# A four-part layer kernel on one core: the feed-forward part's layer norm begun inside the token mixing, its router by blocks, its chosen weights spread by a load

## The reference, cut to what matters

```python
x = x + _L0_attn_ref(_layernorm(x, axis=-1), ...)
x = x + _L0_ffn_ref(_layernorm(x, axis=-1), ...)
...
def _L0_ffn_ref(hidden_states, Wr, br, W1, b1, W2, b2, A1, B1, A2, B2):
    ...
    probs = jax.nn.softmax(x @ Wr + br, axis=-1)
    w, idx = jax.lax.top_k(probs, K)
    combine = jnp.einsum('tk,tke->te', w, jax.nn.one_hot(idx, E, dtype=x.dtype))
    base_h1 = x @ W1 + b1
    t1 = jnp.einsum('td,erd->ter', x, A1)
    l1 = jnp.einsum('ter,efr->tef', t1, B1) * SCALING
    a = gelu_new(base_h1[:, None, :] + l1)
    ca = a * combine[:, :, None]
```

## Time and profile before

| | us |
|---|---|
| median of three executions | 2739.33 |
| lowest, highest | 2738.68, 2741.82 |
| the profiled execution, its time | 2752.23 |
| the profiled execution, its span | 2750.2 |
| busy in the span: PE, DVE | 2630.2 (96%), 2046.9 (74%) |
| busy in the span: ACT, POOL | 1621.7 (59%), 2140.3 (78%) |
| mean granted PE clock | 0.978 of full |

### The profile page before, as it was taken

The page is one execution under the profiler, slowest core; times in us unless marked ns, Lnnn a source line. Parts: engine busy times, 40 slices in busy tenths (PEclk is TensorE's granted clock), DMA queues, the critical chain, the costliest instruction groups (busy, mean ns, idle before and its releaser), DMA issues. The chain is left out here.

```text
span 2750.2 us, 32506 instructions
## 1 busy us (share of the span) xinstructions
PE 2630.2 (96%) x11020; PEld 1874.6 (68%) x11021; DVE 2046.9 (74%) x2916; ACT 1621.7 (59%) x1891; POOL 2140.3 (78%) x1106
## 2 busy tenths in 40 slices
PE   7986999899999999999999999999999999997898
PEld 2333677667777777777777777777777777765665
DVE  6766556578888888888888888888888888886111
ACT  2223323367767776776777677767767767774122
POOL 2543588479988998998899899889989988997233
PEclk9997899999999999999999999999999999999999
DMA  2001456200000000000000000000000000005421
GB/s 68 0 0 53 108 169 167 72 12 5 9 4 20 8 5 16 5 8 5 20 8 5 16 4 9 5 16 8 8 16 4 9 4 9 1 20 142 169 61 46
DMA packets 76126, 90.52 MB, mean 33 GB/s; under 512 B 9310, under 2 KB 64865, under 8 KB 75970
## 3 DMA queue, kind: packets, MB, share of 16 engines
q1 hardware_dynamic: 72994, 81.30, 10.3%
q0 software_dynamic: 2976, 7.22, 0.8%
HBM read 62.39 MB, written 27.02 MB: 33 GB/s over the span
## 5 line engine op out<-in xcount | busy, mean ns | idle before, releaser
L1925 DVE TENSOR_TENSOR at_top<-at_psum_s,at_top 128x512 f32<-128x512 f32 x960 | 662.7, 690 | 215.5 <-ACT at_prob L1832 194.0
L1832 ACT ACTIVATE at_prob<-at_psum_s 128x1024 f32<-128x1024 f32 x512 | 521.4, 1018 | 452.2 <-PE at_psum_s L932 449.0
L2053 POOL TENSOR_TENSOR at_p_lo<-at_prob,at_p_hi 128x1024 fp32r<-128x1024 f32 x256 | 616.3, 2408 | 2.0 <-ACT at_p_hi L1846 2.0
L1914 DVE TENSOR_TENSOR at_prob<-at_prob,at_psum_m 128x1024 f32<-128x1024 f32 x512 | 603.5, 1210 | 0.0
L1838 ACT ACTIVATE at_prob<-at_prob 128x1024 f32<-128x1024 f32 x512 | 537.7, 1050 | 9.9 <-DVE at_prob L1914 6.7
L2082 POOL TENSOR_TENSOR at_acc<-at_acc,at_prob 128x1024 f32<-128x1024 f32 x189 | 453.1, 2397 | 82.8 <-ACT at_prob L1838 73.0
L1747 PE MATMUL at_psum_o<-at_prob,at_v 128*128 128x512 f32 x1024 | 483.4, 594 | 1.8 <-DVE at_oT_lo L1946 1.4
L2086 POOL TENSOR_TENSOR at_acc<-at_acc,at_prob 128x1024 f32<-128x1024 f32 x189 | 454.3, 2404 | 0.0
L930 PE MATMUL at_psum_s<-at_q_hi,sw_gate_up_hi 128*128 128x512 f32 x1024 | 403.4, 394 | 5.1 <-DVE sw_gate_up_lo L1906 5.1
L932 PE MATMUL at_psum_s<-at_q_hi,sw_gate_up_lo 128*128 128x512 f32 x1024 | 401.6, 392 | 0.0
L931 PE MATMUL at_psum_s<-at_q_lo,sw_gate_up_hi 128*128 128x512 f32 x1024 | 401.4, 392 | 0.0
(11 more groups left out here) (350 smaller groups left out, 4486.9 us busy)
## 6 DMA issues: line engine op xcount, KB each, us to landing
ef_gate_up<-in_ef_gate_up SPq DMA_DIRECT2D x8, 1024.0 KB
at_wq_split<-lf_pieces SPq DMA_DIRECT2D x8, 512.0 KB, 2.9
at_wk_split<-lf_pieces SPq DMA_DIRECT2D x8, 512.0 KB, 4.8
at_wv_split<-lf_pieces SPq DMA_DIRECT2D x8, 512.0 KB, 2.9
at_wo_split<-lf_pieces SPq DMA_DIRECT2D x8, 512.0 KB, 4.5
ef_down<-in_ef_down SPq DMA_DIRECT2D x8, 512.0 KB
ef_rows_in<-ef_zeros SPq DMA_DIRECT2D x23, 128.5 KB, 9.0
ef_rows<-ef_rows_in SPq DMA_DIRECT2D x23, 128.5 KB, 2.2
```

The lines of the kernel that those rows point to most:

```text
L1832: nc.scalar.activation(pair(u, c, half), psum_s[:, 2 * half:2 * half + 2, :], ACT.Copy).then_inc(kept, 1)
L1914: nc.vector.tensor_tensor(part, part, psum_m[:].unsqueeze(1).to_broadcast([P, 2, BT]), ALU.subtract).then_inc(shifted, 1)
L1925: nc.vector.tensor_tensor(top[:, u % 2, :], psum_s[:, t, :], top[:, u % 2, :], ALU.max).then_inc(maxed, 1)
L2053: nc.gpsimd.tensor_tensor(p_lo[:, at, :], part, p_hi[:, at, :].bitcast(F32), ALU.subtract).then_inc(p_lo_ready, 1)
```

## The change

The layer norm of blocks 0, 1 and 2 moves into the last three steps of the token mixing, as calls of `BlockNorm`. Statistics of block 0 come at the end of step 3; its deviation, inversion and (on ACT) normalised rows in step 4. The statistics of blocks 1 and 2 come in step 5 on DVE, their deviations on ACT after its loop, their inversions and normalised rows on DVE around the two last `add_out`. The normalised rows lie in the tile that later holds `weights`.

The Block of the layer norm is gone. The router's Block takes block 3's norm, the turns of all blocks, the splits into `x_hi` and `x_lo`, and the router's matmuls by blocks. Four small loads are issued first under a semaphore of their own and seven large ones behind them; POOL splits the router's weights after the small ones and `w1` and `b1t` after the large ones.

`chosen` holds only the one-hot rows. The two chosen weights of each token are turned by one transpose, copied to `weightT` (32 partitions, 128 columns), stored to DRAM by SP as `weight_rows`, and loaded back as two rows of 2048 numbers, each broadcast to 128 partitions. So PE has three spread matmuls per block, not five, and ACT two copies, not four. For blocks 2 and 3 POOL makes the two products with the first hits.

```diff
+    def normalise_on_vector(self, dve, b, rows):
+        nc, ln = self.nc, self.ln
+        dve.wait_ge(ln.rstd_ready, self.stds + b + 1)
+        for j in range(TPB):
+            i = b * TPB + j
+            nc.vector.tensor_scalar(rows[:, j, :], self.x_tok[:, i, :], self.mean_var[:, i, 0:1],
+                                    self.rstd[:, i:i + 1], ALU.subtract, ALU.mult).then_inc(ln.norm_ready, 1)
...
+        eps = next_norm.eps
...
+            next_norm.begin()
...
                         mixes, scans, norms = b < NB, 0 <= a < NB, 0 <= g < NB
+                        if s == NB:
+                            next_norm.deviation(act, 0)
                         for n in range(NM):
...
+                        if s == NB:
+                            next_norm.normalise(act, 0, next_rows(0))
+                    next_norm.deviation(act, 1)
+                    next_norm.deviation(act, 2)
...
                             whole(g)
+                        if s == NB + 1:
+                            next_norm.statistics(dve, 1)
...
                             if norms and n == 0:
                                 centre(g)
+                            if s == NB and n == 1:
+                                next_norm.invert(dve, 0)
+                            if s == NB + 1 and n == 0:
+                                dve.wait_ge(added, 2 * 3)
+                                next_norm.statistics(dve, 2)
...
                                 normalise(g)
                         if scans:
                             own_part(a)
+                        if s == NB - 1:
+                            dve.wait_ge(added, 2)
+                            next_norm.statistics(dve, 0)
+                        if s == NB + 1:
+                            next_norm.invert(dve, 1)
+                            next_norm.normalise_on_vector(dve, 1, next_rows(1))
                         if norms:
                             add_out(g, 0)
+                        if s == NB + 1:
+                            next_norm.invert(dve, 2)
+                            next_norm.normalise_on_vector(dve, 2, next_rows(2))
+                        if norms:
                             add_out(g, 1)
...
-    NQ = 4 * E
+    NQ = 2 * E
...
+                small = (
+                    (router_a1[:], w["lf_router_a1"].rearrange("(c p) n -> p c n", p=P)),
+                    (br[:], w["lf_br"][0, :].partition_broadcast(P)),
+                    (order[:], w["c_order"][0, :].partition_broadcast(P)),
+                    (choose[:], w["c_choose"]),
+                )
...
+                    (b2[:], w["lf_b2"][0, :].partition_broadcast(P)),
+                )
+                N_SMALL = 16 * len(small)
...
+                def turn_psum(b):
+                    return [banks[:, b % 2 * NC + c, :] for c in range(NC)]
+
+                def first_low(b):
+
+                    return "pool" if b >= 2 else "vector"
+
+                def low_done(b):
+                    return sum(2 if first_low(k) == "pool" else 4 for k in range(b + 1))
+
                 with nc.Block() as block:
+                    @block.sync
+                    def _(sp):
+                        for dst, src in small:
+                            sp.dma_start(dst, src).then_inc(small_moved, 16)
+                        for dst, src in loads:
+                            sp.dma_start(dst, src).then_inc(loaded, 16)
+                        sp.wait_ge(small_moved, N_SMALL)
+                        sp.wait_ge(chosen_copied, 1)
+                        sp.dma_start(weight_rows, weightT[:]).then_inc(small_moved, 16)
+                        sp.wait_ge(small_moved, N_SMALL + 16)
+                        flat = weight_rows.rearrange("(j i) p -> j (i p)", j=2)
+                        for j in range(2):
+                            sp.dma_start(weights[:, j, :], flat[j, :].partition_broadcast(P)).then_inc(small_moved, 16)
+                        sp.wait_ge(small_moved, N_SMALL + 48)
+                        sp.wait_ge(loaded, 16 * len(loads))
+
...
+                        pool.wait_ge(small_moved, N_SMALL)
...
+                        pool.wait_ge(loaded, 16 * len(loads))
...
+                        for b in range(NB):
+                            tok = bass.ts(b, BT)
+                            if first_low(b) == "pool":
+                                pool.wait_ge(spread_copied, 2 * b + 1)
+                                pool.wait_ge(t1_lo_ready, b + 1)
+                                nc.gpsimd.tensor_tensor(low_hi[:, 0, tok], t1_hi[:, tok].bitcast(F32), hits[:, 0, tok],
+                                                        ALU.mult).then_inc(split_steps, 1)
+                                nc.gpsimd.tensor_tensor(low_lo[:, 0, tok], t1_lo[:, tok].bitcast(F32), hits[:, 0, tok],
+                                                        ALU.mult).then_inc(split_steps, 1)
...
+                        def turn(b):
+                            if b >= 2:
+                                pe.wait_ge(ln.lo_copied, own_norm.copied + NC * (b - 1))
+                            own_norm.turn(pe, b, own_rows(b), turn_psum(b))
...
+                        def router(b):
+                            pe.wait_ge(ln.lo_copied, own_norm.copied + NC * (b + 1))
+                            if b == 0:
+                                pe.wait_ge(split_steps, 2)
...
+                        turn(0)
+                        turn(1)
+                        router(0)
+                        turn(2)
+                        router(1)
+                        turn(3)
+                        router(2)
+                        router(3)
+                        low_rank(0)
+                        pe.wait_ge(logitsT_copied, NB)
+                        for i in range(NT):
+                            last = nc.tensor.transpose(logits[:, i, :], logitsT[:, bass.ts(i, P)], ident[0:E, 0:E])
+                        last.then_inc(logits_ready, 1)
+                        for b in range(1, NB):
+                            low_rank(b)
                         pe.wait_ge(chosen_ready, 1)
+                        nc.tensor.transpose(banks[0:2 * NT, 0, 0:P], weight[:].rearrange("p j i -> p (j i)"),
+                                            ident[:]).then_inc(chosen_psum, 1)
...
+                            if Q_BANK(b) == 0:
+                                pe.wait_ge(chosen_copied, 1)
...
-                            pe.wait_ge(chosen_copied, 2 * b + 2)
-                            for k in range(5):
-                                n = 5 * b + k
...
+                                    ob, ok = divmod(n - 8, 3)
                                     if ok == 2:
-                                        pe.wait_ge(low_steps, 4 * ob + 4)
+                                        pe.wait_ge(low_steps, low_done(ob))
                                     else:
-                                        pe.wait_ge(spread_copied, 4 * ob + (ok + 1 if ok < 2 else ok))
-                                out = banks[:, (1 + n) % 8, :]
-                                if k < 3:
-                                    last = nc.tensor.matmul(out, choose_r[:, k, :], chosenT_r[:, tok], start=True, stop=True)
-                                else:
-                                    last = nc.tensor.matmul(out, weigh[:, k - 3, :], chosenT[:, tok], start=True, stop=True)
-                                last.then_inc(spread_psum, 1)
+                                        pe.wait_ge(spread_copied, 2 * ob + ok + 1)
+                                nc.tensor.matmul(banks[:, (1 + n) % 8, :], choose_r[:, k, :], chosenT[:, tok],
+                                                 start=True, stop=True).then_inc(spread_psum, 1)
...
+                        own_norm.deviation(act, 3)
+                        own_norm.take_hi(act, 0, turn_psum(0))
+                        own_norm.normalise(act, 3, own_rows(3))
+                        for b in range(1, NB):
+                            own_norm.take_hi(act, b, turn_psum(b))
...
+                        act.wait_ge(chosen_psum, 1)
+                        nc.scalar.activation(weightT[:], banks[0:2 * NT, 0, 0:P], ACT.Copy).then_inc(chosen_copied, 1)
                         for b in range(NB):
-                            tok = bass.ts(b, BT)
-                            act.wait_ge(chosen_psum, b + 1)
-                            for dst in (chosenT, chosenT_r):
-                                nc.scalar.activation(dst[:, tok], banks[0:NQ, Q_BANK(b), :],
-                                                     ACT.Copy).then_inc(chosen_copied, 1)
+                            act.wait_ge(chosen_psum, b + 2)
+                            nc.scalar.activation(chosenT[:, bass.ts(b, BT)], banks[0:NQ, Q_BANK(b), :],
+                                                 ACT.Copy).then_inc(chosen_copied, 1)
...
-                            for k in (0, 1, 3, 4):
-                                n = 5 * b + k
```

(41 more changed lines are left out.)

167 lines of the change are left out of this document (34 added, 133 removed).

## The result

The changed kernel takes 2722.26 us (median of 4 runs, 2721.14 to 2723.30), the kernel before on the same chip 2739.01 (4 runs, 2736.57 to 2741.82): ratio 0.9938, 95% interval 0.9922 to 0.9954. A later pair on another chip (e9) gives 2723.29 against 2738.40, ratio 0.9945 (0.9932 to 0.9958); one of e9's six executions, of 6808 us, is left out of that ratio. The profiled execution of the changed kernel took 2721.14 with a span of 2719.3.

What follows compares the result with a forecast made beforehand. Took a hand-over chain between token mixing and main loop, no engine full, as the bound: 1.8 us later, then 41.5 us where it was 58.0, 14.7 less, 2739.33 to 2724.6; range from 2718.5 to 2732.

Steps and rivals of the forecast that it cites:

- case A: Router chain: DVE waits for POOL's splits of w1 and b1t; 2724.6 us, own range 2722 to 2728, chance 0.58.
- the seam's gain: Third token-mixing step's first residual add to main loop's first matmul, 97.92 us before: claimed 14.7 us less.
- Step 1: Token mixing with the norm inside: ends 1.8 us later, from 0.4, 0.5 and 0.9.
- Step 2: From token mixing's end to the router's logits: logits at about 259.5, 8.1 us earlier than before.
- Step 3: Router chain meeting POOL's splits: two-input DVE instructions wait for whole POOL instructions; chosen_ready at 269.3, bounds 265.5 to 270.8.
- equal sharing: Router chain beside POOL, other reading: chain at most 1.3 us longer, total within 1.5 us of the free-running rival's.
- Step 4, compute: Router's end, turns, spreads and products on PE, ACT, DVE and POOL: from 269.3 to 281.5 to 282.3.
- Step 4, load: Router's end, weights stored and loaded back as two 1 MB broadcasts at 300 GB/s: landed at 281.5.
- C: Weight loads: broadcasts at half rate end last, landing at 288.7; total 2731.3 us, chance 0.12.
- D: Weight loads: landing after 296.7, slower than before; 2752.2 us at 60 GB/s, chance 0.03.
- A sign of being wrong: Main loop's first matmul to the span's end: forecast wrong if its 2453.2 us changed.

Runs made afterwards that it cites:

- e9: Changed kernel run again, unedited, on another chip: 2723.29 us, ratio 0.9945 to the kernel before.
- e1: Kernel before the change run again, unedited, for its profile: 2737.71 us (one run).
- e4: Changed kernel with the norm of blocks 0 to 2 moved out of token mixing to the router's Block: ratio 0.9952 to the kernel before.
- e7: Changed kernel with w1 and b1t loaded and split early, and the norm taken out of token mixing: ratio 0.9966 to the kernel before.
- e2: Changed kernel with w1 and b1t loaded first and split by POOL once those two landed: ratio 0.9922 to the kernel before.
- e3: Changed kernel with the chosen weights spread by matmul again, no store or loads: ratio 0.9978 to the kernel before.
- e5: Changed kernel with POOL's subtraction for w1_lo cut into eight pieces: 2726.94 us (one run).
- e10: Changed kernel with w1 and b1t loaded first and split early, run again: 2718.11 us, ratio 0.9927 to the kernel before.
- e6: Changed kernel with all 16 products on DVE, none on POOL: 2735.92 us (one run).
- e8: Changed kernel with the early w1 and b1t split, and PE spreading block 0 before turning blocks 2 and 3: ratio 0.9914 to the kernel before.

## Why the prediction was right

The forecast was 2724.6, case A; measured is 2722.26. The mechanism of A is what the runs show, and the total is nearer than the sum behind it deserves: it put the seam's gain 1.6 us too high (14.7, measured 13.1), and something outside the seam made up for it ("the total" below). To set a predicted mark against the profile after, 2.78 us are taken off it (199.13-196.35, the drift that e1 shows).

- **Step 1** (1.8 us): 41.71 against 39.91, on the spot. The exactness is luck. The reasons given are there, each smaller: the inversion in step 4 costs 0.25 (0.4), `centre` is a further 0.37 late (0.5), and the last add a further 0.47 (0.9), behind block 2's rows. Most of the rest is one scan in step 4, 2.14 us after and 1.48 before, and the kernel before has it at 2.20 in e1, so it isn't the change's. Over the profiles with the norm inside, the stretch is 40.96 to 42.66, over those without it (e1, e4, e7 and before) 39.88 to 41.56; the means differ by 1.4.
- **Step 2** (logits at 259.5, so 256.7): measured 256.00. The router's first matmul was to start at 246, so 243.2, and did at 243.60, waiting for POOL's split of the router weights as said.
- **Step 3**, the largest unknown: `w_lo` was to end at 263, so 260.2 (260.29); `b1t_lo` at 265.2, so 262.4 (262.65; 242.85+12.6 is 255.45 and not 255.3, which makes it 265.35); `chosen_ready` at 269.3, so 266.5 (266.39+0.17 = 266.56). That rests on one pair of instructions, 1.74 us long, taken to 4.62 us. e2, e3, e5 and e7 agree: the wait goes, moves or shrinks with the overlap. By the Trainium skill's page "SBUF — State Buffer", section "Who interferes with whom", a VectorE instruction with two SBUF inputs and a GpSimd one that reads SBUF exclude each other for a whole instruction; the traces agree at 4.62 and 2.40 us, and equal sharing, which would have made the third instruction about 0.6, is out.
- **Step 4, compute**: end at 281.5 to 282.3, so 278.7 to 279.5; it was 280.85. Two terms were small. From `chosen_ready` to the first product 5.3 us against 4.5, because PE stood 6.36 us waiting for the held-up chain and its 16 turns then took 3.62 at the low level of 1.2 GHz for most of the time (the granted clock is 0.50 in 268 to 269.5). Over the kernels, the same 16 turns take 1.91 us after a pause of 1.78 to 1.97 (e4, e7, e10), 2.74 after 2.45 (e2), and 3.57 to 3.62 after 5.08 to 6.72 (e5, e6, e9 and the changed kernel). The sum had priced the wait on DVE, and not what PE's pause does to PE. And the meetings of DVE's and POOL's products cost 1.7, not 1: 1.35 and 1.75 for two that are 0.69 when free. (POOL's product was put at 1.3 and is 1.27 when free; a quarter of `w_lo`'s 4.62 and a fixed part gives that, not "half its rate".)
- **Step 4, load**: forecast as long as compute (281.5, so 278.7), and it ended at 275.5 or before. The store took 1.4 us, not the bound of 2.9, and 2 MB came at 401 to 431 GB/s, not 300. The rate had been taken from other loads (12.6 us for 3.3 MB), during which the DMA engines were busy too: 239.76 to 252.40 of the kernel before has a DMA share of 0.96 at 288 GB/s. So it wasn't the issuing that kept it low; the engines move these two broadcasts faster than that mix of loads, and why isn't shown. Rivals C and D had this step as theirs, and neither came near. That the load branch was over-priced left the total alone, since the other branch is longer.
- **The total**: the sum was 14.7 us for the seam, measured 13.1 in the first pair and 11.7 in e1 and e9. The medians differ by 16.8 and 15.1. The forecast lies between, because it was compared with a median; that it is within 2.4 of it is in part luck. In every kernel that has a ratio, it says 1 to 7 us more than the seam (e10 has 20.3 against 18.7 to 19.1, e8 23.6 against 16.8 to 17.3, e4 13.2 against 9.4 to 9.8). No stretch outside the seam shows that steadily: attention's first accumulation to the expert part takes 2026.9 us in e9, 2028.4 in the changed kernel, 2036.3 in e2, 2034.5 in e1. But nearly all that differs there is one wait, for the store of the running sum ahead of the expert part. In the kernel before, the changed one, e2 and e10 (line, who waited for what, us, times, longest):
```profile
POOL ef_before L2634 <- DMA ef_tokens<-x_tok: 40.6, 1, 40.6
POOL ef_before L2626 <- DMA ef_tokens<-x_tok: 30.6, 1, 30.6
POOL ef_before L2631 <- DMA ef_tokens<-x_tok: 38.6, 1, 38.6
POOL ef_before L2631 <- DMA ef_tokens<-x_tok: 30.4, 1, 30.4
```
 Less this wait, the stretch is 1996.4 to 1999.5 us in all twelve profiles. The last two lines are one kernel, so the 8 us between them come with the execution; e1 has 36.5, e9 30.5, the others 35.2 to 40.7. Whether the edits make the short wait more frequent can't be told from one or two profiles each, so where the few us of the medians are stays **open**.
- **A sign of being wrong that was met**: from the main loop's first matmul to the span's end it was to stay 2453.2, and it is 2438.1 (2719.3-281.16). The kernel before, again (e1), has 2442.5, and the twelve profiles 2438.1 to 2453.2, so the sign couldn't separate anything; 10.0 of the 15.0 us are the wait above.
- **Where the gain comes from**: the spread by a load 8.7 (e3), the norm inside token mixing 3.3 (e4, of 9.6). If these add, about 1 of 13.1 is left for the turns and the router by blocks, no more than two profiles of one kernel differ by. Undoing that part alone wasn't tried, and the parts needn't add: with the early split the norm inside is worth 13.1 (93.04 against 79.91).

## What to carry to other kernels

A step that is moved ahead meets other neighbours: write down what every engine that can hold it up does at the new time, and move that too (here another load order with its own semaphore was worth another 5 us, and it was worth it only with the norm out of the way). An instruction's length is part of its price: 4.6 us on GpSimd in one piece hold up 0.3 us of VectorE for 3.5. Judge a small edit by a stretch with both edges in untouched work, and not by marks counted from the start of the span.

## What the runs showed of the hardware that was not expected

- **A row of `normalise`, with one large input and its scalars by column, waits as well** (e7: 3.48 us in place of 1.37 for four, and 2.95 for four beside the cast of `w1`; in e4 2.17 beside the split of the router's weights). Step 3 had looked for two inputs in SBUF only. The Trainium skill's page "SBUF — State Buffer", in the same section, says that this kind of instruction can take the pair of ports that the two engines share; the trace agrees, with 3.48 us. Statistics (1.39), reductions (0.28 to 0.29) and the reciprocal (0.25) were never lengthened.
- **The granted clock after the same pause falls into different stretches.** Granted PE clock of 243 to 247, in e3 and then in the changed kernel:
```profile
243.00:247.00 4.00, 3.97 (x23) 2.36 (x24) 2.15 (x4) 1.81 (x4) 0.33 (x1) 1.00 1.02 384
```
```profile
243.00:247.00 4.00, 3.40 (x11) 1.76 (x12) 1.29 (x2) 1.43 (x3) 0.88 (x2) 0.57 1.02 383
```
 The edit of e3 touches nothing before the logits but one more small load. In both kernels PE had paused 1.52 us before its first turns. In e3 those turns ran at the low level, 1.2 GHz (16 in 3.65 us, where the changed kernel took 1.94), while PE had to wait for POOL anyway, and the router's first block at 2.4 GHz (0.40 a matmul, against 0.63). From the router's first matmul to the logits it takes 10.85 us in e3, against 12.40: that is 1.5 of the 2.2 us by which its logits are early, and the rest was there at the last add. It is about the size of what one profile can say of such an edit.
- **Two broadcasts of 8 KB rows to 128 partitions, 2 MB in all, need 5.9 us** from issue to landing, and the loads behind the store of 16 KB were issued 1.44 us after it (267.40 and 268.84), its landing included; in e2 it is 2.39. The nearest row had been 2.9 us for a store of 512 KB.
